# Sum passes of a two-layer graph network by groups of four blocks on one Trainium2 core

## The chip, the cores and the metric

The kernel runs on one core of one Trainium2 chip (trn2). The metric is the device time of one execution in microseconds (us). The engines are called PE (TensorE), DVE (VectorE), ACT (ScalarE), POOL (GpSimd) and SP (SyncE); each has its own instruction stream, and they meet only at semaphores.

## What is computed

12500 nodes with 64 features, 200000 edges (`src`, `dst`, sorted by `dst`). Three layers each sum the neighbours' states over the edges, and a fourth block sums the neighbours' states the other way and three edge features besides. Between them stand small matrix products and layer norms.

```python
def _demo_layer(h, src, dst, deg_pos, inv_deg, Wg, Wl, Ws, b):
    g = h @ Wg
    neigh_mean = jax.ops.segment_sum(h[dst], src, num_segments=h.shape[0]) * inv_deg[:, None]
    extra = neigh_mean @ Wl + h @ Ws
    out = g + deg_pos[:, None] * extra + b
    return jax.nn.elu(out)
...
    target_vec = jnp.concatenate([node_feature[node_j], ef, et], axis=1)
    neighbor_emb = target_vec @ W1.T + b1
    neighbors_sum = jax.nn.relu(jax.ops.segment_sum(neighbor_emb, node_i, num_segments=N))
    out = jnp.concatenate([neighbors_sum, source_node_vec], axis=1) @ W2.T + b2
```

## The kernel before, in words

**Setup.** The edges are ranked and scattered once, so that each block of 128 slots x 4 edges (`K = 4`) belongs to one tile of 128 nodes. There are 544 blocks (`NB`) in each of two orders, by source tile and by destination tile. The node states stay in SBUF in `node`; a state is kept as three bf16 parts side by side (`HW = 192` columns).

**The stages.** After the setup and two wide passes (`wide_by_dst`, `wide_by_src`) the program runs: node layer 1, spread, sums, layer 2, spread, sums, layer 3, spread, sums, spread, sums, and the last node block. A `spread` writes the states of 544 blocks into the table `gathered` in HBM. A `sums` reads them back in the other order and adds them up by node. `sums` is called four times, and it alone is changed, with the `gather` on POOL that feeds it.

**One `sums` stage** loops over 34 turns of 16 blocks (`TURN = 16`), and 4 blocks are a group, so a turn has 4 groups and a stage 136. For each block:
- POOL gathers 128 rows from `gathered` into one of 16 slots of `ring` (L641). It waits at the head of each group for the indices (`sum_idx`) and for each block until PE is done with the slot (`sum_mm`).
- DVE builds the one-hots of the block's slots in one of four buffers `oh_s` by one compare (L1350), three blocks ahead.
- PE multiplies the one-hots with the gathered rows, 4 matmuls (one for each of `K`) that add up in one of four PSUM banks (L818). It waits for `sum_oh`, `sum_got` and `sum_red`, and signals `sum_mm`.
- DVE sums the three parts from PSUM into `red` (L1354, signal `sum_red`) and adds `red` to the node's tile (L1468, signal `sum_add`). Where the tile lies is loaded into registers, eight at a time (L362).

**Beside it, once a group,** a quarter of the edge features is summed in fp32. SP fetches the rows into `frows` (L508). DVE builds their one-hots `foh` by a compare (L1350, called from `sums`) in its step for the first block of the group; ACT casts them to fp32 into `fohf` (L1083), which lies in `hring`, and then copies the next gather indices (L972). PE multiplies behind the fourth block of the group (`feature_sum`, L750, recorded as eight matmuls), and DVE adds the result to the node (L1444) in its step for the third block of the next group.

Nothing is scheduled by a planner: each engine's order is the order of the code, and inside an engine nothing overtakes.

Of the kernel before, what the change touches and what calls it, by code (L numbers as in the profile page):

```python
# [7 lines left out]
ALU = mybir.AluOpType  # L8
ACT = mybir.ActivationFunctionType
AX = mybir.AxisListType  # L10
# [5 lines left out]
P = 128  # L16
D = 64
# [52 lines left out]
def build(nc, x, src, dst, ef, stf, et, Wg1, Wl1, Ws1, b1, Wg2, Wl2, Ws2, b2, Wgo, Wlo, Wso, bo,  # L70
          W1t, c1, W2t, c2, out):
    with ExitStack() as ctx:
# [48 lines left out]
        red = sb("red", [P, 2, D])  # L121
# [76 lines left out]
        foh = sb("foh", [P, P, K], BF16)  # L198
        fohf = hring[:, :, :].rearrange("p s w -> p (s w)").bitcast(F32)[:, 0:K * P].rearrange("p (k n) -> p k n", n=P)
# [112 lines left out]
        class Sum:  # L312
# [3 lines left out]
            def __init__(self, number, k):  # L316
                self.k, self.q0, self.n0 = k, number * NQ, number * NB
                self.f0, self.g0 = number * NQ, (number + 2) * NI
                self.idx, self.got, self.oh = sum_idx, sum_got, sum_oh
                self.mm, self.red, self.add = sum_mm, sum_red, sum_add  # L320
# [242 lines left out]
        def _(pool):  # L563
# [65 lines left out]
            def gather(q, spread):  # L629
# [3 lines left out]
                def body(i, first):  # L633
                    for c in range(TURN):
                        n, g = TURN * i + (q.n0 + c), c // 4
# [17 lines left out]
        def _(pe):  # L653
# [155 lines left out]
            def sums(q):  # L809
                def body(i, first):  # L810
                    for c in range(TURN):
                        n = TURN * i + (q.n0 + c)
                        pe.wait_ge(q.oh, n + 1)
                        pe.wait_ge(q.got[c], 16 * i + (16 * q.g0 + 16))
                        if not first or c > 3:
                            pe.wait_ge(q.red, n - 3)
                        for k in range(K):
                            mm = pe.matmul(ps[:, c % 4, 0:HW], oh_s[:, c % 4, :, k], ring[:, c, k * HW:(k + 1) * HW],  # L818
                                           start=k == 0, stop=k == K - 1)
                        mm.then_inc(q.mm, 1)  # L820
                        if c % 4 == 3:
                            g = c // 4
                            f, u = 4 * i + (q.f0 + g), g % 2
                            pe.wait_ge(feat_ohf, f + 1)
                            pe.wait_ge(feat_row[u], 32 * i + (8 * q.f0 + (g // 2 * 16 + 16)))
                            if q.f0 > 0 or not first or g > 1:
                                pe.wait_ge(feat_add, f - 1)
# [839 lines left out]
```

## Time and profile before

| | |
|---|---|
| time, median of 2 runs | 11977.85 us (11972.17 to 11983.54) |
| profiled execution, its own time | 12008.01 us |
| span of that execution, first to last instruction | 12006.2 us |
| mean granted TensorE clock | 0.856 of 2.4 GHz |
| PE, DVE, POOL, ACT busy | 58%, 55%, 42%, 31% of the span |
| four `sums` stages | 544 blocks each |

Busy times are sums over a span; how full an engine is in one stage is read from a stretch of that stage. PE is the matmul row and PEld the weight loads that overlap it; matmuls are pipelined, and a row "x4" in order of time is four of them merged. In the rows in order of time the bracket is the idle time of the engine just before, with what ended it. "Remote" and "another core or an unknown queue" both mean that a semaphore came from something that the records of the moment do not name.

### The profile page before, as it was taken

How to read it: one execution, taken by the hardware profiler on the slowest of the kernel's cores; microseconds unless marked ns; L12 is line 12 of the kernel's file. 1: busy time of each engine (PE TensorE's matmuls, PEld its weight loads, DVE VectorE, ACT ScalarE, POOL GpSimd, SP SyncE). 2: the span in 40 equal slices, each digit the busy share in tenths (PEclk: the TensorE clock that was granted, in tenths of full speed). 3: DMA queues.
4: the chain of work that ended last, by engine and by line, in shares of the span. 5: the costliest groups of instructions: out<-in, count | busy, mean ns of one | idle time of the engine just before them, and what ended most of it. 6: DMA issues, size and time to landing. Idle time of an engine off the chain costs nothing.

```text
span 12006.2 us, 213561 instructions
## 1 busy us (share of the span) xinstructions
PE 7020.0 (58%) x46640; PEld 6056.7 (50%) x46640; DVE 6572.9 (55%) x19818; ACT 3664.2 (31%) x10935; POOL 5053.8 (42%) x4833
## 2 busy tenths in 40 slices
PE   7999998000049997545565555555536555655556
PEld 6898886000038886444344444444434444444445
DVE  8459998000046665444675456655567555665546
ACT  0003332000037775333571115811139211571111
POOL 0018888666644444554015550055500455215550
PEclk9999999999999998666797777977769777897776
DMA  9905555565569997455495564955629655885560
GB/s 385 366 20 144 145 144 142 137 148 137 144 194 304 301 301 225 142 142 135 165 346 161 164 164 155 358 164 163 160 52 395 201 163 160 269 333 161 164 161 18
DMA packets 1567398, 2320.70 MB, mean 193 GB/s; under 512 B 974516, under 2 KB 1046056, under 8 KB 1567320
## 3 DMA queue, kind: packets, MB, share of 16 engines
q1 hardware_dynamic: 1227608, 1356.73, 33.5%
q0 software_dynamic: 292608, 911.36, 27.5%
q10 hardware_dynamic: 47104, 51.75, 1.8%
q8 instruction: 27, 0.44, 0.0%
q14 instruction: 51, 0.42, 0.0%
HBM read 1328.55 MB, written 986.78 MB: 193 GB/s over the span
## 4 chain that ended last, share of the span: by engine, by line
PE 28%; issue 25%; DVE 19%; another core or an unknown queue 13%; ACT 7%; DVEq 4%; DMA 3%; ACTq 1%; POOL 0%; SPq 0%; POOLq 0%
PE ps L750 10%; PE ps L818 5%; PE ps L703 4%; DVE mask L1319 3%; DVE oh_s L1350 3%; ACT ring L1059 3%; DMA gathered<-ring 2%; PE ps L738 2%; ACT hring L1069 2%; PE ps L743 2%; DVE prod L1303 2%; PE ps L787 2%; DVEq L362 1%; DVE ohj L1209 1%
## 5 line engine op out<-in xcount | busy, mean ns | idle before, releaser
L641 POOL DMA_INDIRECT ring<-gathered,gidx x2176 | 2089.5, 960 | 3930.5 <-DMA gathered<-ring 2098.6
L571 POOL DMA_INDIRECT by_src<-prow,ppos x1562 | 1924.9, 1232 | 1485.5 <-DMA ppos<-pos 940.6
L818 PE MATMUL ps<-ring,oh_s 128*128 128x192 bf16 x8704 | 1217.8, 294 | 1797.3 <-DVE oh_s L1350 1585.3
L1354 DVE TENSOR_REDUCE red<-ps 128x64 f32<-128x192 f32 x2720 | 957.1, 352 | 2351.2 <-remote 1285.1
L818 PEld LDWEIGHTS ps<-ring,oh_s 128*128 128x128 bf16 x8704 | 918.6, 127 | 2059.2 <-DVE oh_s L1350 961.0
L1083 ACT CAST hring<-foh 128x512 f32<-128x512 bf16 x544 | 361.2, 664 | 3585.7 <-DVE foh L1350 3065.2
L1432 DVE CAST ring<-ps 128x384 bf16<-128x384 f32 x2176 | 1126.8, 553 | 328.1 <-PE ps L743 274.1
L743 PE MATMUL ps<-hring,oht_g 128*128 128x192 bf16 x8704 | 941.8, 246 | 544.7 <-DVE ring L1432 150.1
L750 PE MATMUL ps<-frows,hring 128*128 128x193 f32 x4352 | 1182.6, 433 | 4.2 <-issue 3.9
L1059 ACT CAST ring<-ps 128x384 bf16<-128x384 f32 x2176 | 1138.4, 524 | 10.1 <-PE ps L743 9.8
L1350 DVE TENSOR_TENSOR oh_s<-loc,iota_loc 128x512 bf16<-128x512 bf16 x2720 | 1126.5, 414 | 5.3 <-ACT loc L1027 3.1
L743 PEld LDWEIGHTS ps<-hring,oht_g 128*128 128x128 fp8e4 x8704 | 654.2, 97 | 832.2 <-issue 803.5
L721 PE MATMUL ps<-snap,oht_e 98*128 98x98 f32 x3130 | 1057.0, 441 | 0.0
L738 PE MATMUL ps<-ident_bf,oh 128*128 128x128 bf16 x2176 | 211.4, 220 | 1410.1 <-DVE oh L1350 1410.0
L750 PEld LDWEIGHTS ps<-frows,hring 128*128 128x128 f32 x4352 | 1008.9, 260 | 39.1 <-issue 6.8
L738 PEld LDWEIGHTS ps<-ident_bf,oh 128*128 128x128 bf16 x2176 | 167.9, 114 | 1410.7 <-issue 1410.6
L956 ACT COPY snap<-ps 98x98 f32<-98x98 f32 x1565 | 378.2, 242 | 1641.2 <-PE ps L718 1180.6
L1069 ACT COPY hring<-node 128x192 bf16 x2176 | 860.6, 396 | 55.3 <-issue 51.3
L750 PE MATMUL ps<-rows,ohf 128*128 128x193 f32 x4352 | 849.4, 339 | 26.6 <-ACT ohf L983 22.8
L604 POOL DMA_INDIRECT rows<-by_src,gidx x544 | 517.7, 952 | 727.3 <-PE ps L750 269.9
L721 PEld LDWEIGHTS ps<-snap,oht_e 98*128 98x128 f32 x3130 | 820.5, 323 | 0.0
L1338 DVE MEMSET node<- 128x64 f32 x1 | 0.1, 112 | 1356.1 <-DMA by_src<-prow,ppos 1356.1
(217 smaller groups left out, 12841.3 us busy)
## 6 DMA issues: line engine op xcount, KB each, us to landing
gathered<-ring SPq DMA_DIRECT2D x544, 768.0 KB
by_src<-zeros SPq DMA_DIRECT2D x34, 6272.0 KB, 45.5
frows<-by_src SPq DMA_DIRECT2D x544, 392.0 KB
oht_g<-oht SPq DMA_DIRECT2D x544, 256.0 KB, 5.4
gathered<-got SPq DMA_DIRECT2D x136, 776.0 KB
prow<-in_edge_attr_n SPq DMA_DIRECT2D x284, 352.0 KB
bc<-tidrow ACTq DMA_DIRECT2D x313, 160.0 KB
prow<-in_edge_attr SPq DMA_DIRECT2D x142, 352.0 KB
```

The source lines that it names most:

```text
L571: pool.indirect_dma_start(out=table, out_offset=bass.IndirectOffsetOnAxis(ap=ppos[:, s, j:j + 1], axis=0), in_=prow[:, s, j, :], in_offset ...
L641: pool.indirect_dma_start(out=ring[:, c, :], out_offset=None, in_=gb, in_offset=offsets(g, c % 4)).then_inc(q.got[c], 16)
L721: pe.matmul(where, oht_e[0:T, v, l * P:(l + 1) * P], snap[0:T, (u * LANES + l) % 2, :], start=True, stop=False, skip_group_check=True).the ...
L738: mm = pe.transpose(to[:, k * P:(k + 1) * P], one_hots[:, :, k], ident_bf[:, :])
L743: mm = pe.matmul(ps[:, bank + k // 2, k % 2 * HW:(k % 2 + 1) * HW], eight(one_hots)[:, k * P:(k + 1) * P], parts, start=True, stop=True, s ...
L750: mm = pe.matmul(ps[:, bank, 0:FEAT], one_hots[:, k, :], rows_of[:, k, 0:FEAT], start=k == 0, stop=k == K - 1)
L818: mm = pe.matmul(ps[:, c % 4, 0:HW], oh_s[:, c % 4, :, k], ring[:, c, k * HW:(k + 1) * HW], start=k == 0, stop=k == K - 1)
L1059: act.copy(ring[:, c, 0:2 * HW], ps[:, 2 * (c % 4), 0:2 * HW]).then_inc(q.g, 1)
L1069: act.copy(hring[:, e, :], parts_at(at[e])).then_inc(q.hc, 1)
L1350: return dve.tensor_tensor(to, loc[k][:, bass.ds(b * K, K)].unsqueeze(1).to_broadcast([P, P, K]), iota_loc[:, :, :], ALU.is_equal)
L1354: return dve.tensor_reduce(red[:, u], ps[:, bank, 0:HW].rearrange("p (a d) -> p d a", d=D), AX.X, ALU.add)
L1432: dve.tensor_copy(ring[:, c, 2 * HW:4 * HW], ps[:, 2 * (c % 4) + 1, 0:2 * HW]).then_inc(q.gv, 1)
```

## The change

The sum passes go by groups. `red` becomes two times four parts. Instead of four compares, four sums of parts and four PE signals, a group has one each. The one-hots of blocks move from `oh_s` to `oht_g` (`ohq`, two halves of four blocks); `oh_s` becomes free for two `foh` buffers and for the second of two `fohf`. PSUM banks 0 and 1 hold one group, 2 and 3 the next. One semaphore per group (`sum_got[::4]`) counts the four gathers. POOL waits for the slots once a group.

```diff
@@ buffers
-        red = sb("red", [P, 2, D])
...
-        foh = sb("foh", [P, P, K], BF16)
-        fohf = hring[:, :, :].rearrange("p s w -> p (s w)").bitcast(F32)[:, 0:K * P].rearrange("p (k n) -> p k n", n=P)
+        red = sb("red", [P, 2, 4, D])
+        ohq = oht_g[:, :, :].rearrange("p b s -> p (b s)").rearrange("p (e n k) -> p e n k", n=P, k=K)
+        foh = [oh_s[:, 2], oh_s[:, 3]]
+        fohf = [flat_of[:, 0:K * P].rearrange("p (k n) -> p k n", n=P) for flat_of in
+                (hring[:, :, :].rearrange("p s w -> p (s w)").bitcast(F32),
+                 oh_s[:, 0:2].rearrange("p a n k -> p (a n k)").bitcast(F32))]
@@ gather, POOL
                         if c % 4 == 0:
                             pool.wait_ge(q.idx, 4 * i + (q.q0 + g + 1))
-                        if not first:
-                            pool.wait_ge(q.mm, n - (TURN - 1))
+                            if not first:
+                                pool.wait_ge(q.mm, 4 * i + (q.q0 + g - 3))
...
-                                                in_offset=offsets(g, c % 4)).then_inc(q.got[c], 16)
+                                                in_offset=offsets(g, c % 4)).then_inc(q.got[g], 16)
@@ sums, PE
-                    for c in range(TURN):
-                        n = TURN * i + (q.n0 + c)
-                        pe.wait_ge(q.oh, n + 1)
-                        pe.wait_ge(q.got[c], 16 * i + (16 * q.g0 + 16))
-                        if not first or c > 3:
-                            pe.wait_ge(q.red, n - 3)
-                        for k in range(K):
-                            mm = pe.matmul(ps[:, c % 4, 0:HW], oh_s[:, c % 4, :, k], ring[:, c, k * HW:(k + 1) * HW],
-                                           start=k == 0, stop=k == K - 1)
+                    for g in range(4):
+                        m, f, u = 4 * i + (q.q0 + g), 4 * i + (q.f0 + g), g % 2
+                        pe.wait_ge(q.oh, m + 1)
+                        pe.wait_ge(q.got[g], 64 * i + (q.g0 + 64))
+                        if not first or g > 1:
+                            pe.wait_ge(q.red, m - 1)
+                        for e in range(4):
+                            c = 4 * g + e
+                            for k in range(K):
+                                mm = pe.matmul(ps[:, 2 * u + e // 2, e % 2 * 256:e % 2 * 256 + HW], ohq[:, c % 8, :, k],
+                                               ring[:, c, k * HW:(k + 1) * HW], start=k == 0, stop=k == K - 1,
+                                               skip_group_check=True)
                         mm.then_inc(q.mm, 1)
...
+                        pe.wait_ge(feat_ohf, f + 1)
+                        pe.wait_ge(feat_row[u], 32 * i + (8 * q.f0 + (g // 2 * 16 + 16)))
+                        if q.f0 > 0 or not first or g > 1:
+                            pe.wait_ge(feat_add, f - 1)
+                        feature_sum(4 + u, fohf[u], frows[:, u]).then_inc(feat_mm, 1)
@@ sums, ACT
-                        if q.f0 > 0 or not first or g > 0:
-                            act.wait_ge(feat_mm, f)
-                        act.copy(fohf, foh[:, :, :].rearrange("p n k -> p k n")).then_inc(feat_ohf, 1)
+                        if q.f0 > 0 or not first or g > 1:
+                            act.wait_ge(feat_mm, f - 1)
+                        act.copy(fohf[g % 2], foh[g % 2][:, :, :].rearrange("p n k -> p k n")).then_inc(feat_ohf, 1)
@@ sums, DVE
+                def ones(m, g):
+                    places = loc[q.k][:, bass.ds(m * (4 * K), 4 * K)].rearrange("p (e k) -> p e k", k=K)
+                    dve.tensor_tensor(ohq[:, 4 * (g % 2):4 * (g % 2) + 4], places.unsqueeze(2).to_broadcast([P, 4, P, K]),
+                                      iota_loc[:, :, :].unsqueeze(1).to_broadcast([P, 4, P, K]),
+                                      ALU.is_equal).then_inc(q.oh, 1)
...
+                        dve.wait_ge(q.mm, m + 1)
+                        dve.tensor_reduce(
+                            red[:, u], ps[:, 2 * u:2 * u + 2, :].rearrange("p b (h c) -> p (b h) c", c=256)[:, :, 0:HW]
+                            .rearrange("p e (a d) -> p e d a", d=D), AX.X, ALU.add).then_inc(q.red, 1)
+                        if not (last and g > 1):
+                            ones(4 * i + (g + 2), g)
+                        if q.f0 > 0 or not first or g > 1:
+                            dve.wait_ge(feat_ohf, f - 1)
+                        one_hots(foh[u][:, :, :], 1, f).then_inc(feat_oh, 1)
+                        dve.wait_ge(q.red, m + 1)
+                        for e in range(4):
+                            n = TURN * i + (q.n0 + 4 * g + e)
+                            if not first or g + e > 0:
+                                dve.wait_ge(q.add, n)
+                            to = node_at(at[4 * u + e], A0, D)
+                            dve.tensor_tensor(to, to, red[:, u, e], ALU.add).then_inc(q.add, 1)
+                        if not first or g > 0:
+                            features(f - 1, 1 - u, at_f[g - 1 if first else g], q.f0 == 0 and first and g == 1)
```

On PE, in the looped turn of the first `sums` stage, the second group of a turn stands like this before, with the features of the group (L750) behind its four blocks and each block waiting for its own signals:

```order
L813 REGISTER_ALU
L818 MATMUL ps<-ring,oh_s 128x192 [waits sum_red,sum_got4,sum_oh]
L818 MATMUL ps<-ring,oh_s 128x192 x3
L813 REGISTER_ALU
L818 MATMUL ps<-ring,oh_s 128x192 [waits sum_red,sum_got5,sum_oh]
L818 MATMUL ps<-ring,oh_s 128x192 x3
L813 REGISTER_ALU
L818 MATMUL ps<-ring,oh_s 128x192 [waits sum_red,sum_got6,sum_oh]
```

And so the same group in the changed kernel, with the features (L755) and the next group behind it:

```order
L821 REGISTER_ALU [waits sum_got4,sum_oh]
L825 MATMUL ps<-ring,oht_g 128x192 [waits sum_red]
L825 MATMUL ps<-ring,oht_g 128x192 x15
L755 MATMUL ps<-frows,oh_s 128x193 [waits feat_add,feat_row1,feat_ohf]
L755 MATMUL ps<-frows,oh_s 128x193 x3
L825 MATMUL ps<-ring,oht_g 128x192 [waits sum_red,sum_got8,sum_oh]
L825 MATMUL ps<-ring,oht_g 128x192 x15
```

The four waits of a group have become one, ahead of 16 matmuls in a row; the features stand behind the group and ahead of the next one in both.

On DVE, the head of a group in the looped turn of a later `sums` stage is this before; the first compare is that of `foh`, the second that of a block's one-hots:

```order
L1354 TENSOR_REDUCE red<-ps 128x64 [waits sum_mm]
L1458 REGISTER_ALU
L1350 ISA [waits feat_ohf]
L1350 TENSOR_TENSOR foh<-loc,iota_loc 128x512
L1350 ISA
L1350 TENSOR_TENSOR oh_s<-loc,iota_loc 128x512
L1468 ISA [waits sum_add,sum_red]
L1468 TENSOR_TENSOR node<-node,red 128x64
```

After the change the head of a group is this; the compare into `oht_g` is that of four blocks, the one into `oh_s` that of `foh`:

```order
L1462 TENSOR_REDUCE red<-ps 128x256 [waits sum_mm]
L1443 ISA
L1443 TENSOR_TENSOR oht_g<-loc,iota_loc 128x2048
L1354 ISA [waits feat_ohf]
L1354 TENSOR_TENSOR oh_s<-loc,iota_loc 128x512
L1474 REGISTER_ALU [waits sum_red]
L1476 ISA [waits sum_add]
L1476 TENSOR_TENSOR node<-node,red 128x64
```

The wait for `sum_mm` was that for the first block of the group and is now that for all four, and `foh` stands behind the reduce and the compare of four blocks.

## Rows read from the trace of the kernel before

**Rows 1.** The page, its head: span, busy time and share of each engine.
```profile
span 12006.2 us, 213561 instructions
...
PE 7020.0 (58%) x46640; PEld 6056.7 (50%) x46640; DVE 6572.9 (55%) x19818; ACT 3664.2 (31%) x10935; POOL 5053.8 (42%) x4833
```

**Rows 2.** Busy time by stretches: first and last `sums` stage, third node layer.
```profile
core 0: us, PE busy (x) PEld busy (x) DVE busy (x) ACT busy (x) POOL busy (x), PEclk, DMA share, GB/s
...
6266.00:7253.00 987.00, 552.03 (x3267) 478.94 (x3268) 508.20 (x1905) 106.75 (x276) 501.62 (x525) 0.74 0.57 159
...
10736.00:11722.00 986.00, 548.18 (x3231) 476.18 (x3231) 495.98 (x1880) 101.43 (x265) 516.80 (x538) 0.73 0.58 162
...
8763.00:9010.00 247.00, 77.05 (x410) 69.75 (x410) 159.86 (x307) 100.87 (x182) 0.00 (x0) 0.61 0.12 37
```

**Rows 3.** Groups by line within 700 us of the first `sums` stage.
```profile
L1350 DVE TENSOR_TENSOR oh_s<-loc,iota_loc 128x512 bf16<-128x512 bf16 x385 | 159.6, 414 | 0.0
...
L1354 DVE TENSOR_REDUCE red<-ps 128x64 f32<-128x192 f32 x385 | 135.4, 352 | 304.6 <-remote 145.5 <-PE ps L818 111.0 <-issue 47.9
...
L1083 ACT CAST hring<-foh 128x512 f32<-128x512 bf16 x96 | 63.7, 664 | 625.4 <-DVE foh L1350 534.1 <-issue 91.2
```

**Rows 4.** In order of time, a turn of that stage: start, length, engine, line.
```profile
6700.52 0.66 ACT L1083 CAST hring<-foh 128x512 f32<-128x512 bf16 x1 [9.80 <-DVE foh L1350]
...
6700.87 0.35 DVE L1354 TENSOR_REDUCE red<-ps 128x64 f32<-128x192 f32 x1
...
6701.50 2.84 PE L750 MATMUL ps<-frows,hring 128*128 128x193 f32 x8
...
6701.61 0.35 DVE L1354 TENSOR_REDUCE red<-ps 128x64 f32<-128x192 f32 x1
...
6702.14 0.97 POOL L641 DMA_INDIRECT ring<-gathered,gidx  x1 [4.74 <-PE ps L818]
...
6703.41 0.95 POOL L641 DMA_INDIRECT ring<-gathered,gidx  x1 [0.30 <-issue]
...
6704.13 2.80 PE L818 MATMUL ps<-ring,oh_s 128*128 128x192 bf16 x16
...
6706.72 1.58 PE L750 MATMUL ps<-frows,hring 128*128 128x193 f32 x8
...
6708.15 1.15 PE L818 MATMUL ps<-ring,oh_s 128*128 128x192 bf16 x12
...
6711.13 0.95 POOL L641 DMA_INDIRECT ring<-gathered,gidx  x1 [0.30 <-issue]
...
6713.73 0.36 DVE L1354 TENSOR_REDUCE red<-ps 128x64 f32<-128x192 f32 x1 [5.02 <-remote]
```

**Rows 5.** Busy time and clock in three short stretches of that turn.
```profile
6700.00:6704.00 4.00, 3.12 (x12) 3.01 (x13) 3.16 (x13) 0.76 (x2) 1.56 (x2) 0.50 0.24 86
6707.00:6709.00 2.00, 2.00 (x19) 1.95 (x19) 1.71 (x7) 0.00 (x0) 1.35 (x2) 1.00 0.61 209
6714.00:6718.00 4.00, 3.18 (x12) 3.01 (x13) 3.36 (x14) 0.76 (x2) 1.63 (x2) 0.50 0.39 111
```

**Rows 6.** The chain that ended last, in order of time, within that turn.
```profile
6704.34 0.65 PE ps L818 x4
...
6708.71 5.00 another core or an unknown queue
```

**Rows 7.** In order of time: the SyncE queue, and the next run of gathers.
```profile
6713.86 0.33 SPq L508 DMA_DIRECT2D frows<-by_src  x1
...
6716.07 0.98 POOL L641 DMA_INDIRECT ring<-gathered,gidx  x1 [3.99 <-PE ps L818]
...
6727.83 0.35 DVE L1444 TENSOR_TENSOR node<-node,ps 128x193 f32 x1 [2.29 <-remote]
```

**Rows 8.** Groups by line over the whole span, DVE operations of other sizes.
```profile
L1276 DVE TENSOR_TENSOR cmp<-iota_row,thr 99x512 f32<-99x512 f32 x272 | 188.2, 692 | 274.5 <-PE ps L703 274.5
...
L1416 DVE TENSOR_TENSOR node<-node,ps 128x1 f32 x544 | 79.9, 147 | 0.2 <-issue 0.2
...
L1494 DVE TENSOR_REDUCE nm<-oht_g 128x7 f32<-128x448 f32 x28 | 17.4, 622 | 1.0
```

More of the change, by code:

```diff
@@ L1435, in sums, with features @@
             def sums(q):
-                def ones(b, c):
-                    one_hots(oh_s[:, c % 4], q.k, b).then_inc(q.oh, 1)
-                def features(f, u, at):
+                def ones(m, g):
[3 more added lines that the diff above has]
+                                      ALU.is_equal).then_inc(q.oh, 1)
+                def features(f, u, at, first):
                     dve.wait_ge(feat_mm, f + 1)
-                    if not (isinstance(f, int) and f == 0):
+                    if not first:
                         dve.wait_ge(feat_add, f)
@@ L1446, in body @@
                 def body(i, first, last=False):
-                    at_f = tiles(1, 4 * i + q.f0, 4, mybir.EngineType.DVE)
-                    for half in range(2):
-                        at = tiles(q.k, TURN * i + 8 * half, 8, mybir.EngineType.DVE)
-                        for e in range(8):
-                            c = 8 * half + e
-                            n = TURN * i + (q.n0 + c)
-                            f, g = 4 * i + (q.f0 + c // 4), c // 4
-                            dve.wait_ge(q.mm, n + 1)
-                            parts_summed(c % 2, c % 4).then_inc(q.red, 1)
-                            if c % 4 == 0:
-                                if q.f0 > 0 or not first or g > 0:
-                                    dve.wait_ge(feat_ohf, f)
-                                one_hots(foh[:, :, :], 1, f).then_inc(feat_oh, 1)
-                            if not (last and c > TURN - 4):
-                                ones(TURN * i + (c + 3), c + 3)
-                            if c % 4 == 2 and g > 0:
-                                features(f - 1, (g - 1) % 2, at_f[g - 1])
-                            dve.wait_ge(q.red, n + 1)
-                            if not first or c > 0:
-                                dve.wait_ge(q.add, n)
-                            to = node_at(at[e], A0, D)
-                            dve.tensor_tensor(to, to, red[:, c % 2], ALU.add).then_inc(q.add, 1)
@@ L1469, in body @@
-                    features(4 * i + (q.f0 + 3), 1, at_f[3])
-                for b in range(3):
-                    ones(b, b)
+                    at_f = tiles(1, q.f0 if first else 4 * i + (q.f0 - 1), 4, mybir.EngineType.DVE)
+                    for g in range(4):
+                        m, f, u = 4 * i + (q.q0 + g), 4 * i + (q.f0 + g), g % 2
+                        if u == 0:
+                            at = tiles(q.k, TURN * i + 4 * g, 8, mybir.EngineType.DVE)
+                        dve.wait_ge(q.mm, m + 1)
[11 more added lines that the diff above has]
+                            if not first or g + e > 0:
+                                dve.wait_ge(q.add, n)
+                            to = node_at(at[4 * u + e], A0, D)
+                            dve.tensor_tensor(to, to, red[:, u, e], ALU.add).then_inc(q.add, 1)
+                        if not first or g > 0:
+                            features(f - 1, 1 - u, at_f[g - 1 if first else g], q.f0 == 0 and first and g == 1)
@@ L1472, in sums @@
+                for m in range(2):
+                    ones(m, m)
                 body(0, True)
@@ L1475, in sums @@
                 body(NI - 1, False, True)
+                at_f = tiles(1, q.f0 + NQ - 4, 4, mybir.EngineType.DVE)
+                features(q.f0 + NQ - 1, 1, at_f[3], False)
                 dve.wait_ge(q.add, NB + q.n0)
+                dve.wait_ge(feat_add, q.f0 + NQ)
             def spread_over(ap):
```

21 lines of the change are left out of this document (6 added, 15 removed).

## The prediction

> **What bounds the kernel now.** I read the page first, then the busy time by stretches, the groups of instructions inside one aggregation stage, and last two turns of that stage in order of time. The page gives a span of 12006.2 us, with no engine above 58% [rows 1]: nothing is full, so the time lies in waits between engines. The change touches only `sums`, which runs four times. The stretches [rows 2] show the first and the last of those stages alike: of 987 and 986 us PE is busy 552 and 548 us (56%), DVE and POOL about half, and the granted TensorE clock is 0.74 and 0.73. Since only 1.2 and 2.4 GHz are ever granted, a mean of 0.74 is some 48% of the time at 2.4 GHz.
>
> The groups in 700 us of the first stage [rows 3] give the pace: 96 casts of the feature one-hots on ACT, one for each group of four blocks, so 700/96 = 7.29 us a group. There are 4 stages x 136 groups = 544 groups; their 544 x 7.3 = 3970 us are a third of the span. In a group POOL issues 4 gathers in steps of 1.25 to 1.27 us [rows 4], 5.0 us; DVE has four steps of 0.73 and two instructions of some 0.35 more, 3.6 us. Both would allow a shorter group than 7.3.
>
> What fills it can be read in order of time [rows 4]. DVE's step for one block is reduce, one-hot, add, 0.73 us (6700.87 to 6701.61). PE's features at 1.2 GHz take 2.63 us (6701.50 to the next product at 6704.13); at 2.4 GHz they take 1.43 us (6706.72 to 6708.15), and a product 0.082 us instead of 0.16. That the clock is 0.50 there and 1.00 later stands in the stretches of a few us [rows 5]. Then comes a gap that no engine accounts for: PE's last product record begins before 6709.3, yet DVE's reduce, which waits only for PE's signal, begins at 6713.73 after 5.02 us. The chain calls the releaser unknown [rows 6], and the SyncE queue, which waits for the signal of the features that started at 6706.72, issues its next DMA at 6713.86 [rows 7]. All that time POOL had gathers running: it began at 6702.14, issued eight, the last at 6711.13. The product that ended at 6704.99 was answered at once [rows 6], those behind it late. The second run of gathers shows the same: begun at 6716.07, a late signal, of the features, seen at 6727.83 [rows 7]. I read this as: PE's signals are prompt in the first 3 us or so of a run of gathers, and are held after that until the run has nearly landed, 2.6 us after its last one began (6713.73 less 6711.13). The mechanism is not visible; the pattern is.
>
> **The change part by part.** On DVE four reduces become one of 768 inputs (L1462), four compares one of 2048 elements (L1443); the four adds, the feature compare and the feature add stay. PE signals once a group, POOL waits once a group, and PSUM and one-hots hold two groups. The price of the new operations:
> - Reduce: 192 inputs take 352 ns [rows 3] and 448 take 622 ns [rows 8], 1.055 ns more for each, so 768 take 0.96 us against 4 x 0.35. Bounds: 0.9 to 1.41 (four old ones).
> - Compare: a one-element add takes 147 ns [rows 8]; 512 bf16 elements take 414 [rows 3], so 0.52 ns an element and 1.22 us for 2048, against 4 x 0.41. If the four-level pattern lost that rate it would go by the fp32 compare, 692 ns for 512 (1.06 ns each, [rows 8]): 2.33 us. I take 1.22, since types and innermost run are those of before.
> - The saved signals and fixed parts, some 0.7 us of DVE a group, are work on an engine that waits half of the time: nothing by themselves. The moves of `foh` and `fohf` into other tiles and the second buffer of each cost nothing; neither does the single wait of POOL, whose 0.30 us between gathers is there when it waits for nothing [rows 4].
>
> **What the new order makes of it.** The products are said to run two groups ahead, and `oh` and PSUM would allow it. But the order of PE is products m, features m, products m+1, and features m wait for `feat_ohf`, which ACT makes from `foh`, and DVE makes `foh` of group m only behind its wait for the products of the same group m, and now behind the large reduce and the large compare. Before, DVE made it after the first block of the group, and PE still had three blocks, whose cover the change takes away. So PE is never ahead, and a group is one chain without overlap: products m, signal, reduce, compare, `foh`, ACT's cast, features m, products m+1. Its links, from [rows 4] where not priced above:
> - DVE and ACT: reduce 0.88 and compare 1.14 (each less the 0.08 by which the next one overlaps), `foh` 0.42, cast 0.66, and hand-overs 0.02 + 0.04 + 0.05: 3.2 us.
> - PE at 1.2 GHz: features 2.63, products 4 x 0.65 [rows 6] = 2.60, and 0.2 from the last product's turn to its signal: 5.4. At 2.4 GHz: 1.43 + 16 x 0.082 = 1.31 + 0.2: 2.95.
> - So a group is 8.6 us at 1.2 GHz and 6.15 at 2.4 GHz, if signals are prompt.
> - The held signals: ACT copies the next indices right behind the cast; POOL's first gather starts 0.96 us after the cast's end (6701.18 to 6702.14). The signal of the next products is due 5.45 us after the cast at 1.2 GHz, 4.5 into POOL's run, and 3.0 at 2.4 GHz, 2.0 into it. The first falls where signals were held. A run is now four gathers, 3 x 1.25 us from first start to last start, and over 2.6 later: 6.35. That holds the slow case's signal another 1.85: 10.45 us. The fast case is not held. Bounds for the hold: 0 to 3 us.
>
> Which clock? PE would be busy 5.2 of 10.45 us in the slow case and 2.75 of 6.15 in the fast one, about 48%. The busy share and the clock go together in the trace: 56% with 0.74, and 77 of 247 us, 31%, with 0.61 [rows 2]. Between them 48% gives 0.70, 40% of the time at 2.4 GHz. The mean group is then 1/(0.6/10.45 + 0.4/6.15) = 8.17 us. Against 7.29 this is 0.88 us more, x 544 = 479 us. Nothing outside `sums` changes. The profiled execution took 12008.0 us, 30 above the median of 11977.9: 12008 + 479 - 30 = 12,457, I say 12,460 us.
>
> **The rivals.**
> - *Full clock throughout.* What speaks for it: at 2.4 GHz PE's idle piece is only 3.2 us a group, shorter than the one of over 4.5 us behind which the clock fell [rows 4, 5], and all of PE's work of a group is in one piece. Against it: PE is busy less than now, and a lower share goes with a lower clock [rows 2]. Each group takes 6.15: 544 x -1.14 = -620, 11,360 us. It decides from about three quarters of the time at 2.4 GHz, where the group is 6.85. The Trainium skill (TensorE: Matmul & The Clock Gate, HAM oscillation) says that gaps in the matmuls are what brings the clock down, and by that rule this rival gains; the gap of this trace, from before 6709.3 until the clock is back at 0.50, agrees, and no row here has a steady train of 3.2 us ones. Chance 0.17.
> - *Signals not held.* Runs of four with a pause, and a quarter of PE's signals, may keep every signal prompt. Then 1/(0.6/8.6 + 0.4/6.15) = 7.41 us, +65: 12,040 us, no change. For it: the first signals of both runs were prompt. Against it: 4.5 us into a run none is seen prompt. Chance 0.21.
> - *Compare at the fp32 rate.* The chain gets 1.11 longer: 9.28 us, 13,060 us. Chance 0.07.
> - *Clock at 1.2 GHz throughout.* 10.45 us a group, 13,690 us. Chance 0.07.
> - That it does what its name says, PE really ahead by two groups, would leave POOL's 5.0 us as the bound and give -1200. The order of instructions excludes it.
>
> **How the numbers follow.** My forecast, the chain at mixed clock with held signals, has 0.48; its own range is 12,200 to 12,850. Measurement can tell about 2%, 240 us. Faster: the first rival and a little from the second's lower edge, 0.20. Within 2%: most of the second and the low edge of the forecast, 0.21. Slower: the rest, 0.59. The range reaches down to 11,550, half of the first rival, and up to 13,300, past the slow compare; outside are some 0.09 and 0.07.
>
> **What would show it.** In the changed profile: no products of a group before the features of the last one; ACT's cast waiting for DVE's `foh`, and PE's features waiting for the cast, in every group; casts every 8 us rather than 7.3; the compare at 1.2 us and the reduce at 0.96; POOL in runs of four with pauses of 3 us; a mean clock near 0.70; the spread and node stages unchanged. I am wrong if PE's features do not wait for the cast, if groups come under 7 us, or if the clock is above 0.85 in these stages.

## The result, and the profile after

The changed kernel took 12,493.19 us (two runs, 12,484.01 to 12,502.37) where the kernel before took 11,977.85: a ratio of 1.043, 95% interval 1.0385 to 1.0475, slower. The forecast was 12,460 us, a ratio of 1.040, by +0.88 us a group. The profiled execution took 12,484.01 us. It is the first case forecast, slower, and 33 us from the median; but two of its terms were wrong, in opposite directions, and the experiments below are there to separate them.

The head of the page of the kernel after, and its row for the gathers, against [rows 1]:

```profile
span 12482.2 us, 198644 instructions
...
PE 7395.1 (59%) x46640; PEld 6501.7 (52%) x46640; DVE 6479.0 (52%) x16554; ACT 3659.7 (29%) x10935; POOL 5028.2 (40%) x4833
...
L646 POOL DMA_INDIRECT ring<-gathered,gidx x2176 | 2063.1, 948 | 4474.9 <-DMA gathered<-ring 2129.8
```

There are 14,917 instructions fewer, and DVE is busy 94 us less. PE, with exactly as many matmuls as before, is busy 375 us longer: they ran at a lower clock. Busy time by stretches for the first and the last `sums` stage of the kernel after, as in [rows 2]:

```profile
6224.00:7211.00 987.00, 589.11 (x2901) 526.33 (x2900) 430.10 (x961) 89.25 (x240) 456.51 (x483) 0.71 0.48 145
11100.00:12087.00 987.00, 585.81 (x2894) 523.01 (x2895) 431.87 (x967) 90.00 (x242) 456.60 (x482) 0.71 0.48 145
```

In as many microseconds PE gets through 2901 recorded matmuls where it had 3267. The groups by line, kernel after, 6400 to 7100 us, as in [rows 3]:

```profile
L755 PE MATMUL ps<-frows,oh_s 128*128 128x193 f32 x344 | 119.7, 525 | 137.5 <-ACT oh_s L1088 134.3 <-issue 3.2
...
L1443 DVE TENSOR_TENSOR oht_g<-loc,iota_loc 128x2048 bf16<-128x2048 bf16 x86 | 104.6, 1216 | 0.0
L1462 DVE TENSOR_REDUCE red<-ps 128x256 f32<-128x768 f32 x86 | 82.4, 958 | 360.1 <-PE ps L825 211.8 <-issue 148.4
```

86 groups in 700 us are 8.14 us each; over a whole stage, from its first cast to its last, the groups of the four stages take 8.25, 8.23, 8.26 and 8.24 us, where before they took 7.31, 7.34, 7.34 and 7.33. 544 groups by 0.91 us are 495 us, and that is the whole difference (476 between the two profiled executions, 515 between the medians). The new operations cost what was forecast: the compare 1.216 us, the reduce 0.958. PE now waits for ACT's cast, which it did not before. And DVE's reduce waits for nothing that is unknown: the 145.5 us of "remote" in [rows 3] are gone.

In order of time, kernel after, two groups (start, length, engine, line, and in brackets the idle time before):

```profile
6706.42 2.91 PE L755 MATMUL ps<-frows,hring 128*128 128x193 f32 x8 [3.46 <-ACT hring L1088]
...
6707.12 0.95 POOL L646 DMA_INDIRECT ring<-gathered,gidx  x1 [3.00 <-ACT gidx L977]
...
6709.12 2.77 PE L825 MATMUL ps<-ring,oht_g 128*128 128x192 bf16 x16
...
6710.87 0.95 POOL L646 DMA_INDIRECT ring<-gathered,gidx  x1 [0.30 <-issue]
6711.93 0.96 DVE L1462 TENSOR_REDUCE red<-ps 128x256 f32<-128x768 f32 x1 [4.92 <-issue]
6712.80 1.22 DVE L1443 TENSOR_TENSOR oht_g<-loc,iota_loc 128x2048 bf16<-128x2048 bf16 x1
6713.94 0.42 DVE L1354 TENSOR_TENSOR oh_s<-loc,iota_loc 128x512 bf16<-128x512 bf16 x1
...
6714.39 0.65 ACT L1088 CAST oh_s<-oh_s 128x512 f32<-128x512 bf16 x1 [8.12 <-DVE oh_s L1354]
...
6715.09 2.78 PE L755 MATMUL ps<-frows,oh_s 128*128 128x193 f32 x8 [3.20 <-ACT oh_s L1088]
...
6717.67 1.99 PE L825 MATMUL ps<-ring,oht_g 128*128 128x192 bf16 x16
...
6719.69 0.96 DVE L1462 TENSOR_REDUCE red<-ps 128x256 f32<-128x768 f32 x1 [3.75 <-PE ps L825]
...
6723.05 2.91 PE L755 MATMUL ps<-frows,hring 128*128 128x193 f32 x8 [3.39 <-ACT hring L1088]
```

This is the serial chain of the forecast, link by link. Features 2.70 us (6706.42 to 6709.12; forecast 2.63), products and their signal 2.81 (forecast 2.80), reduce to features 3.16 (6711.93 to 6715.09; forecast 3.2): 8.67 us from features to features, where the forecast had 8.6 for a group at 1.2 GHz with prompt signals. The signal comes 4.8 us into POOL's run of four, where the forecast had it held by 1.85 us. It was not held: the reduce begins as soon as PE's last product is over (6709.12 + 2.77 = 6711.89, and 6711.93). So it is all through this stage: in 128 of 129 groups between 6240 and 7300 us the reduce begins 0.04 us after the end of the last product's record. The next group, 6715.09 to 6723.05, takes 7.96.

The clock of the same two groups, by stretches of the kernel after (PE busy is the second number, the granted clock the third from the end):

```profile
6703.00:6706.30 3.30, 0.00 (x0) 0.00 (x0) 3.01 (x6) 0.74 (x2) 0.94 (x1) 0.81 0.74 253
6706.40:6709.10 2.70, 2.68 (x8) 2.56 (x9) 0.57 (x2) 0.00 (x0) 1.67 (x2) 0.50 0.14 24
6709.10:6711.90 2.80, 2.79 (x17) 2.27 (x15) 0.00 (x0) 0.00 (x0) 2.11 (x3) 0.51 0.76 238
6712.00:6715.00 3.00, 0.00 (x0) 0.00 (x0) 2.71 (x5) 0.61 (x2) 0.00 (x0) 1.00 0.41 139
6715.10:6717.60 2.50, 2.50 (x8) 2.40 (x9) 0.70 (x3) 0.03 (x1) 1.31 (x2) 0.54 0.00 0
6717.70:6719.60 1.90, 1.90 (x17) 1.67 (x15) 0.00 (x0) 0.00 (x0) 1.42 (x2) 0.74 0.74 142
```

Here is the second thing that the forecast had wrong. The mean is 0.71 (forecast 0.70), but the full clock falls mostly on the stretches in which PE waits (1.00 from 6712 to 6715, with no matmul at all), and the low one on those in which it works. Laid over PE's matmul records of the stage (6224 to 7211 us), the clock record is at 2.4 GHz in 81% of PE's idle time and in 15% of its busy time; in the kernel before (6266 to 7253) it is at 2.4 GHz in 43% of the busy time. The mean while PE works has fallen from 0.71 to 0.58, while the mean over the whole stretch has only fallen from 0.74 to 0.71. Of the 128 groups from 6240 to 7300, 77 take 7.6 to 8.2 us and 51 take 8.7 to 8.9; none is near the 6.15 us that I had given to 40% of the time.

### The profile page after: what moved, and what is told of

Same layout as the page of the kernel before. It is cut to its first block, busy times and chain, and to the rows that moved or that the text cites. A ratio compares the mean times of both kernels' runs of the same rounds, so it can differ in the third digit from the quotient of the medians.

```text
span 12482.2 us, 198644 instructions
## 1 busy us (share of the span) xinstructions
PE 7395.1 (59%) x46640; PEld 6501.7 (52%) x46640; DVE 6479.0 (52%) x16554; ACT 3659.7 (29%) x10935; POOL 5028.2 (40%) x4833
## 4 chain that ended last, share of the span: by engine, by line
PE 32%; issue 31%; DVE 17%; ACT 7%; DMA 4%; DVEq 3%; another core or an unknown queue 3%; ACTq 1%; POOL 0%; SPq 0%; POOLq 0%
PE ps L755 13%; PE ps L825 6%; PE ps L708 4%; DMA gathered<-ring 4%; DVE mask L1323 3%; PE ps L743 3%; ACT ring L1064 2%; DVE oh_s L1354 2%; PE ps L748 2%; ACT hring L1074 2%; PE ps L792 2%; DVE prod L1307 1%; DVE ohj L1213 1%; PE ps L670 1%
## 5 line engine op out<-in xcount | busy, mean ns | idle before, releaser
L1462 DVE TENSOR_REDUCE red<-ps 128x256 f32<-128x768 f32 x544 | 521.1, 958 | 2347.6 <-PE ps L825 1523.6
L755 PE MATMUL ps<-frows,hring 128*128 128x193 f32 x2176 | 754.8, 525 | 927.3 <-ACT hring L1088 900.3
L825 PE MATMUL ps<-ring,oht_g 128*128 128x192 bf16 x8704 | 1257.7, 324 | 53.8 <-DMA ring<-gathered,gidx 53.8
L755 PE MATMUL ps<-frows,oh_s 128*128 128x193 f32 x2176 | 741.2, 516 | 913.4 <-ACT oh_s L1088 887.7
L1436 DVE CAST ring<-ps 128x384 bf16<-128x384 f32 x2176 | 1094.0, 552 | 360.0 <-PE ps L748 332.7
L748 PE MATMUL ps<-hring,oht_g 128*128 128x192 bf16 x8704 | 886.5, 247 | 598.9 <-DVE ring L1436 219.1
L825 PEld LDWEIGHTS ps<-ring,oht_g 128*128 128x128 bf16 x8704 | 1138.2, 139 | 194.3 <-issue 145.7
L755 PEld LDWEIGHTS ps<-frows,hring 128*128 128x128 f32 x2176 | 624.8, 312 | 993.8 <-issue 979.8
L755 PEld LDWEIGHTS ps<-frows,oh_s 128*128 128x128 f32 x2176 | 603.9, 303 | 989.9 <-ACT oh_s L1088 962.5
L755 PE MATMUL ps<-rows,ohf 128*128 128x193 f32 x4352 | 846.8, 338 | 27.9 <-ACT ohf L988 23.8
L1088 ACT CAST oh_s<-oh_s 128x512 f32<-128x512 bf16 x272 | 176.4, 648 | 2091.3 <-DVE oh_s L1354 2091.3
```

Of the source, the lines that this page charges most:

```text
L748: mm = pe.matmul(ps[:, bank + k // 2, k % 2 * HW:(k % 2 + 1) * HW], eight(one_hots)[:, k * P:(k + 1) * P], parts, start=True, stop=True, s ...
L755: mm = pe.matmul(ps[:, bank, 0:FEAT], one_hots[:, k, :], rows_of[:, k, 0:FEAT], start=k == 0, stop=k == K - 1)
L825: mm = pe.matmul(ps[:, 2 * u + e // 2, e % 2 * 256:e % 2 * 256 + HW], ohq[:, c % 8, :, k], ring[:, c, k * HW:(k + 1) * HW], start=k == 0, ...
L1436: dve.tensor_copy(ring[:, c, 2 * HW:4 * HW], ps[:, 2 * (c % 4) + 1, 0:2 * HW]).then_inc(q.gv, 1)
L1462: dve.tensor_reduce(red[:, u], ps[:, 2 * u:2 * u + 2, :].rearrange("p b (h c) -> p (b h) c", c=256)[:, :, 0:HW] .rearrange("p e (a d) -> p ...
```

## The experiments

One thing must be said first: the runs were made in four sessions, and the kernel before did not take the same time in all of them. In two sessions (e1 to e4; e10 and r4) it took 10,502.52 and 10,502.45 us; in the two others (r1, r2, e5, e6; e7 and e8) 11,984.12 and 12,015.88, as in the result above. I call the first two sessions A and the other two B. A kernel is compared only with the kernel before of its own session.

**e1, session A.** `foh` of group f+1 is built in the step of group f, so PE's features never wait for the reduce and the compare of their own group.

```
-  if q.f0 > 0 or not first or g > 1:
-      dve.wait_ge(feat_ohf, f - 1)
-  one_hots(foh[u][:, :, :], 1, f).then_inc(feat_oh, 1)
+  if not (last and g == 3):
+      if q.f0 > 0 or not first or g > 0:
+          dve.wait_ge(feat_ohf, f)
+      one_hots(foh[1 - u][:, :, :], 1, f + 1).then_inc(feat_oh, 1)
...
+  one_hots(foh[0][:, :, :], 1, q.f0).then_inc(feat_oh, 1)
```

> The changed kernel, in which DVE builds the feature one-hots of group m+1, not of group m, in its step for group m. Nothing is left out. Chain theory: features m no longer wait for anything that comes behind products m, so a group falls from 8.2 us to what is next, a run of four gathers with the held signal behind it, about 6.6 us: 544 x (6.6 - 8.2) = -870, about 11,620 us. If no signal is held, PE and POOL set it at 5.3 us: about 10,900. Rival (the large DVE operations or the lower clock cost the time, not the order): unchanged, 12,490 us within 1%.

Measured: 10,674.20 us (four runs), ratio to before 1.0157, interval 1.014 to 1.0174. The 11,620 us that I had expected counted on late signals, of which session A shows none; without them I had expected 10,900. **e2, session A**, leaves `foh` in its group but moves its two statements ahead of the large reduce, directly behind the wait for the products:

```
   dve.wait_ge(q.mm, m + 1)
+  if q.f0 > 0 or not first or g > 1:
+      dve.wait_ge(feat_ohf, f - 1)
+  one_hots(foh[u][:, :, :], 1, f).then_inc(feat_oh, 1)
   dve.tensor_reduce(
...
   ones(4 * i + (g + 2), g)
-  if q.f0 > 0 or not first or g > 1:
-      dve.wait_ge(feat_ohf, f - 1)
-  one_hots(foh[u][:, :, :], 1, f).then_inc(feat_oh, 1)
```

> The changed kernel, in which the feature one-hots of group m stand ahead of the large reduce and the large compare of the same step, still behind the wait for products m. Nothing is left out. Chain theory: the chain of a group gets shorter by the reduce and the compare, 0.88 + 1.14 = 2.0 us, in the slow case from 10.45 to 8.4, in the fast one to the 5.3 us of POOL and PE; mean near 6.5: about 11,570 us. Rival (order does not matter): 12,490 us.

Measured: 10,684.47 us (one run). Groups by line of e1, 5800 to 6500 us:

```profile
L646 POOL DMA_INDIRECT ring<-gathered,gidx x497 | 527.6, 1062 | 173.7 <-issue 146.4 <-PE ps L825 22.1 <-ACT gidx L977 5.2
...
L1443 DVE TENSOR_TENSOR oht_g<-loc,iota_loc 128x2048 bf16<-128x2048 bf16 x122 | 148.7, 1218 | 0.0
...
L755 PE MATMUL ps<-frows,oh_s 128*128 128x193 f32 x488 | 113.5, 385 | 15.3 <-DVE node L1452 9.3 <-ACT hring L1088 3.4 <-issue 2.6
```

122 groups in 700 us, 5.74 each; in this row PE's wait for the cast has shrunk from 134 us to 3.4. Over whole stages the groups of e1 take 5.78 to 5.86 us. With all the rest of the change kept (one reduce, one compare, one signal a group), moving `foh` alone takes 2.4 us off each group, against the 8.17 of the changed kernel on such a chip (r4 below). So nearly all of the loss lies in where `foh` stands, and not in the large operations or the rarer signals: e1 takes back 1312 of the 1484 us by which the changed kernel is slower in session A. The other 172 us, 1.6%, remain, and no run here says what they are; the nearest bound is POOL, at (1.062 + 0.30) x 4 = 5.45 us a group.

**e3, session A**: the kernel before with the gathers of the `sums` stages left out (`gather` does nothing, PE and ACT do not wait for it). **e10**, the same kernel in another session A. **e4, session A**: the changed kernel with the same left out. The sums are then of what happens to be in the ring. The lines below are those of e4.

```
   def gather(q, spread):
-      ...
+      pass
...
-  pe.wait_ge(q.got[g], 64 * i + (q.g0 + 64))
...
-  act.wait_ge(q.got[g], 64 * i + (q.g0 + 64))
+  act.wait_ge(q.idx, 4 * i + (q.q0 + g + 1))
```

> The kernel before without the gathers of its four sum stages: POOL issues none, nobody waits for one, and the products use what lies in the ring. All other work stays. Theory of held signals: without gathers PE's signals are prompt, the 5 us gaps go, and a group falls from 7.3 to about 4.6 us (DVE's 3.6 as the floor, PE's chain of 5.0 at the low clock): 544 x -2.7 = -1,470, about 10,500 us. Rival (the gaps have another cause, such as a change of PE's clock): about 11,980 us, gaps of 3 to 5 us before DVE's reduce still there.

> The changed kernel without the gathers of its four sum stages, in the same way. Theory: the chain without overlap stays, only the hold of up to 1.85 us in the slow case goes: 8.2 becomes about 7.4 us a group, about 12,060 us, and by no means under 6.15 us a group (11,380). It is then slower than the kernel before without gathers by 2.8 us a group, 1,500 us. Rival (the changed kernel is slow because of held signals): it falls as far as the kernel before, to 10,500.

> The kernel before without the gathers of its four sum stages, once more, since e3 ran on a chip on which the signals were not late in the first place. On a chip of the slower kind (kernel before at 11,980 us): theory of signals held while gathers land: without gathers a group takes the same 4.3 us as in e3, 544 x (4.3 - 7.34) = -1,650, about 10,330 us. Rival (the slower chip's PE is late by itself): the group stays well over 5 us and the kernel over 10,800. On a chip of the faster kind: 9,820 again.

Measured: e3 9822.32 us, groups of 4.28 us, 680 less than before; e10 9827.37, 675 less. e4 11,944.29 us, 42 less than r4. e4 by stretches and by line:

```profile
6000.00:6700.00 700.00, 418.52 (x2059) 374.37 (x2058) 304.43 (x680) 63.26 (x170) 0.00 (x0) 0.71 0.16 49
```

```profile
L742 PE MATMUL ps<-frows,oh_s 128*128 128x193 f32 x344 | 119.6, 525 | 137.5 <-ACT oh_s L1074 137.5
...
L1448 DVE TENSOR_REDUCE red<-ps 128x256 f32<-128x768 f32 x85 | 81.4, 958 | 355.6 <-PE ps L811 355.6
```

Without a single gather the changed kernel has the same pace (8.17 us), the same clock and the same wait of PE for the cast, 137.5 us. I had expected the groups to shorten when the gathers went; that theory fell here. By itself e4 speaks for session A alone; that there was no hold in the result either is read from its own trace, above. For the same reason e3 and e10 do not test whether gathers make signals late: the 1470 us that I had expected e3 to save were late signals, and no trace of session A has them. e3 gives an estimate for the group of the kernel before in session A, of which there is no trace: 4.28 + (10,502 - 9822)/544 = 5.5 us, if all of the difference lies in the `sums` stages.

**r4, session A**: the changed kernel itself.

> The changed kernel, unchanged. On a chip of the slower kind 12,490 again. On a chip of the faster kind (kernel before at 10,500 us), where it was not yet run: the chain does not depend on the chip, 8.2 us a group as in e4, about 11,960 us, 14% slower than the kernel before there. Rival (the chain gains from that chip as much as the kernel before): 10,950.

Measured: 11,986.48 us against 10,502.45, one run each: 14.1% slower, groups of 8.15 to 8.19 us. The change costs 544 x 2.7 us there and 544 x 0.9 here. The groups of the changed kernel hardly differ between the sessions (8.17 and 8.24 us); it is the kernel before whose groups are so much shorter in A (some 5.5 us against 7.33). So the forecast of 4% could be right only where the kernel before has its late signals.

**r1 and r2, session B**: both kernels once more, where the kernel before took as long as in the result.

> The kernel before, unchanged, for its trace on the chip of these runs, where its median was 10,502 us and not 11,978. Theory: what is different is the held signals. If they are missing here, DVE's reduce is not late by 3 to 5 us, and a group of a sum stage takes about 5.4 us in place of 7.3 (4 x 136 x 1.9 = 1,030 us of the 1,475 less), with the rest in the two wide passes; engine durations are the same. Rival: the chip's engines or DMA are simply faster, every stage shorter in the same ratio of 0.877.

> The changed kernel, unchanged, on the same chip as the others. Chain theory: a group is the chain of products, reduce, compare, foh, cast and features and hardly depends on gathers or on held signals; it took 8.2 us without gathers, so it takes about 8.25 us here too and the kernel about 12,000 us, 14% slower than the kernel before on the same chip. Rival (both are limited by the same thing and 4% is the price everywhere): 10,950 us.

Measured: before 11,991.73, after 12,499.23 (four runs), ratio 1.0428, interval 1.041 to 1.0445: the result again. Both expectations had counted on a session like A, so that r2 came out 500 us above its own, nearly all of it ahead of the `sums` stages. The waits of r1, 6400 to 7100 us (total, times, longest):

```profile
DVE red L1354 <- remote: 128.6, 29, 5.5
DVE node L1444 <- remote: 102.3, 22, 5.4
```

The late signals of [rows 3, 6, 7] are there again, 231 us in 96 groups. In the traces of e1, e2 and r4 from session A there are none within the `sums` stages.

**e5, session B**: the changed kernel, with 16 products of constants behind each group's products, into a PSUM bank that nothing reads, so that PE has work while it would wait for the cast.

```
   mm.then_inc(q.mm, 1)
+  for k in range(16):
+      pe.matmul(ps[:, 6, 0:HW], ident_bf[:, :], iota_loc[:, 0:HW // K, :].rearrange("p n k -> p (n k)"),
+                start=True, stop=True, skip_group_check=True)
   pe.wait_ge(feat_ohf, f + 1)
```

> The changed kernel with 16 more matmuls a group into an unused PSUM bank, on constants, between the products and the wait for the feature one-hots, so in time in which PE idles. Clock theory: the mean group of 8.2 us lies between a chain of 8.7 at 1.2 GHz and 6.2 at 2.4 GHz; if the extra work keeps the clock at 2.4 GHz a group takes about 6.4, 544 x -1.8 = -980 against the changed kernel on the same chip, about 11,000. Rival (the clock is set otherwise or does not matter): not faster, up to 0.3 us a group slower where the extra matmuls do not fit the gap.

Measured: 11,825.29 us (one run): 674 less than r2 and 1.3% less than before, by adding work. e5 by stretches, and in order of time:

```profile
6400.00:7100.00 700.00, 492.05 (x4071) 457.54 (x4069) 365.19 (x816) 75.87 (x204) 409.58 (x409) 0.90 0.60 172
```

```profile
6504.55 2.83 PE L755 MATMUL ps<-frows,hring 128*128 128x193 f32 x8 [2.14 <-issue]
...
6507.17 1.92 PE L825 MATMUL ps<-ring,oht_g 128*128 128x192 bf16 x16
...
6508.93 1.48 PE L830 MATMUL ps<-iota_loc,ident_bf 128*128 128x192 bf16 x16
...
6512.28 1.57 PE L755 MATMUL ps<-frows,oh_s 128*128 128x193 f32 x8 [1.88 <-ACT oh_s L1091]
...
6513.70 1.48 PE L825 MATMUL ps<-ring,oht_g 128*128 128x192 bf16 x16
```

Both kinds of group stand in these rows: features and products in 4.5 us, and in 2.9. Of 108 groups from 6300 to 7050, 64 take 6.1 to 6.3 us and 38 take 7.7 to 8.1. So the 6.15 us of the forecast for a group at 2.4 GHz is the right price of a thing that the changed kernel does not reach by itself. I had expected nearly all groups there, 6.4 us in the mean, and 11,000 us; a third of them stay slow. PE still stands idle some 2 us a group; that this is why is not shown.

**e6, session B**: in the kernel before, only `foh` is moved, from the first block of a group to the last (`if c % 4 == 0:` becomes `if c % 4 == 3:`).

> The kernel before with one move: DVE builds the feature one-hots of a group in its step for the last block of the group, not for the first. Nothing is left out, and no operation changes its size. Chain theory: the missing cover alone makes it slow: products of the last blocks, signal, reduce, foh, cast and features stand in a row, some 6.9 us at 1.2 GHz and 4.4 at 2.4 GHz where the four products are done at once, near 6.5 us a group with the mixed clock, +550 to +600 us against the kernel before on this chip (11,080). Rival (only the large operations cost): no change, 10,500.

Measured: 12,107.90 us (one run), +124, 0.23 us a group, a quarter of what I had expected from the numbers of session A. Its waits, 6400 to 7100 us:

```profile
PE ps L750 <- ACT hring L1083: 216.6, 88, 4.6
DVE red L1354 <- PE ps L818: 210.4, 77, 4.1
```

PE's wait for the cast appears, 2.5 us in 88 groups, as in the changed kernel. But the waits of the reduce for "remote" have nearly gone in exchange (3.6 us, against 128.6 in r1). The chain is longer, and the late signals that it replaces can have paid for most of it. The change costs 0.9 us a group in B and 2.7 in A, so the same exchange seems to hide a large part of its cost too.

**e8, session B**: the kernel of e1 again. **e7, session B**: the same, with the large compare cut into four of 512 elements, one ahead of each add.

```
+  if not (last and g > 1):
+      ones(4 * i + (g + 2), g, [e])       # one block's 512 elements
   to = node_at(at[4 * u + e], A0, D)
   dve.tensor_tensor(to, to, red[:, u, e], ALU.add).then_inc(q.add, 1)
```

> e1 with one more edit: the compare of 2048 elements is four of 512 again, one ahead of each add of a part. Nothing is left out. Theory: e1's group of 5.8 us is POOL's pace, 4 gathers of 1.25 us plus 0.47 us for each one that a compare of 2048 covers (1418 against 945 ns), while gathers beside a compare of 512 took 987 ns in the kernel before. Short compares then give 5.2 to 5.4 us a group on the faster chip: 10,400 us, 1% under the kernel before and 2.5% under e1. On the slower chip, where signals set the pace, e7 and e8 within 1%. Rival (the longer gathers come from the traffic of the DMA engines): e7 not faster than e8 anywhere.

> The kernel of e1 once more, beside e7. On a chip like that of e1 (kernel before at 10,500 us): 10,675 as then. On a chip like that of the first comparison (kernel before at 11,980 us), where PE's signals are late while gathers land: the lost cover is back, so a group falls well under the changed kernel's 8.24 us; each signal can cost until the run of four gathers has landed, 6.4 us after its start, so a group is 6.4 to 7.3 us and the kernel 11,480 to 11,980. Rival (the chain is not the cause): 12,490 there.

Measured: e7 11,475.52 us (four runs), ratio to before 0.9554, interval 0.9538 to 0.957; e8 11,486.53. Both have groups of 6.40 us. They beat the kernel before by 4.5% and, by the ratios to it, the changed kernel by some 8%; so at the pace of the result, too, the loss is gone when `foh` is built ahead. That they differ by 0.1% says that the length of the compare does not matter in B. Why 6.4 here and 5.8 in A, with the same kernel? First e8, then e1, in order of time:

```profile
6501.76 2.66 PE L825 MATMUL ps<-ring,oht_g 128*128 128x192 bf16 x16
...
6504.53 0.95 POOL L646 DMA_INDIRECT ring<-gathered,gidx  x1 [0.30 <-issue]
...
6507.10 0.96 DVE L1462 TENSOR_REDUCE red<-ps 128x256 f32<-128x768 f32 x1 [4.27 <-remote]
```

```profile
6208.76 2.75 PE L825 MATMUL ps<-ring,oht_g 128*128 128x192 bf16 x16 [3.81 <-DMA ring<-gathered,gidx]
...
6210.62 0.95 POOL L646 DMA_INDIRECT ring<-gathered,gidx  x1 [0.30 <-issue]
...
6211.55 0.96 DVE L1462 TENSOR_REDUCE red<-ps 128x256 f32<-128x768 f32 x1 [3.89 <-PE ps L825]
```

In e8 PE is done at 6504.42 and DVE learns of it at 6507.10, 2.57 us after the last gather of the run began; the forecast read 2.6 off the kernel before. Of the 67 reduces between 6266 and 7090 us before which DVE stood idle for over 2 us, 55 waited for such a signal, and in the median they began 2.56 us after the start of the latest gather. In e1, also within a run of gathers, PE is done at 6211.51 (6208.76 + 2.75), and DVE starts at 6211.55. So late signals exist, in sessions B and with long runs of gathers, and in e1 runs as long have none.

## Why the prediction was right, and where it was not

- *PE is not ahead, and a group is one chain*: right. Between 6400 and 7100 us after the change the cast waits for `foh` in all 86 groups, and PE waits for the cast in 84 of 85. e1 takes `foh` out of the chain, e2 moves it ahead of the reduce and the compare, and the loss is gone but for 1.6 to 1.7% (in B, with e8, it becomes a gain of 4.4%).
- *Prices on DVE*, 0.96 and 1.22 us: measured 0.958 and 1.216. The rival with the compare at the fp32 rate was never in play.
- *Links at 1.2 GHz, 8.6 us*: measured 8.67. *At 2.4 GHz, 6.15*: e5's short groups take 6.1 to 6.3.
- *The held signals*: wrong. "That holds the slow case's signal another 1.85: 10.45 us" should have been 0, within the bounds of 0 to 3. "The first falls where signals were held" took a time within a run of eight and applied it to a run of four with a pause behind it. The result's own trace shows the signal at once in 128 of 129 groups, and e4, in session A, no difference without gathers. The rival "signals not held" had this right, and its 7.41 us a group was too low for the other reason, the clock.
- *Which clock*: the mean was right (0.71 for 0.70) and its use wrong. "40% of the time at 2.4 GHz" was shared out over whole groups, fast ones of 6.15 and slow ones. But a mean over time counts the stretches in which PE idles at the full clock. PE had the full clock in 15% of its busy time only. In most groups the features took the 2.7 us of 1.2 GHz, in a fifth of them 2.0 to 2.2; the products took from 1.6 us, near the full clock, to 2.8. No group had both short, so the groups took 7.6 to 8.2 or 8.7 to 8.9 us. PE's busy share was 59 to 60%, not 48%: the hold, which would have been idle time, was missing (5.2 of 8.6 us are 60%), and the slow matmuls filled more of each group. Here a higher share went with a lower clock, against the line that the forecast drew through [rows 2].
- The two errors: with no hold and the forecast's clock, 7.41; with no hold and the clock as it was, 8.24; with both as forecast, 8.17. The total came out right because they cancel. The order of operations and its prices were foreseen; that the sum met the measured time within 33 us was luck.
- *POOL in runs of four with pauses of 3 us*: right, 3.00 to 4.2 us.
- *Full clock throughout*: PE had a gap of some 3.3 us in each group, and the full clock in 15% of its busy time; in e5, where the gaps are some 2 us, it had it in 73% (6300 to 7050 us, the added products included), and gained 674 us. The Trainium skill (TensorE: Matmul & The Clock Gate, HAM oscillation) says that gaps in the matmuls bring the clock down. The trace agrees with that direction, but not with what the forecast drew from it, that this rival gains with gaps of 3.2 us. This rival was given 0.17; its price was right (e5's short groups), its condition not met.

What stays open: why signals are late in sessions B and prompt in sessions A. Within B the lateness goes with gathers in long runs (there in before, r1, e7, e8; not in after, hardly in e6), but the gathers were never taken out in a session B, so that they cause it is argued, not shown. Neither is it known whether A and B are a property of the chip: the results number the chip 5 and 11 in the sessions A, and 15 and 11 in the sessions B, so if the same number means the same chip, one chip has shown both. e7 was not run in a session A, where POOL is the limit and short compares may help; e1 with the idea of e5 was not tried.

## What to carry to other kernels

When operations of several blocks are merged, look for the small step that another engine waits for between them: merged or not, it should not stand behind the large ones, and is best built one group ahead. Running ahead is only real if every producer in the ring is ahead: here one-hots and products were, and the feature one-hot pulled them all back into one chain. And do not turn a mean granted clock into a share of fast work, before looking in which stretches the engine works.

## What was not expected of the hardware

**Two kinds of sessions.** The kernel before took 10,502 us in some and 11,984 or 12,016 in others, 14% apart, with every single run within 0.2% of its session's median. In the changed kernel (11,986 against 12,493) 457 of the 507 us lie ahead of the first cast of the first `sums` stage, which is at 5747 us in A and at 6204 in B.

**Gathers wait for large compares.** A gather's issue takes 0.95 us alone. From e2 in order of time:

```profile
6205.49 1.22 DVE L1443 TENSOR_TENSOR oht_g<-loc,iota_loc 128x2048 bf16<-128x2048 bf16 x1
6205.87 1.65 POOL L646 DMA_INDIRECT ring<-gathered,gidx  x1 [0.30 <-issue]
...
6210.09 1.22 DVE L1443 TENSOR_TENSOR oht_g<-loc,iota_loc 128x2048 bf16<-128x2048 bf16 x1
...
6210.43 1.70 POOL L646 DMA_INDIRECT ring<-gathered,gidx  x1 [0.30 <-ACT gidx L977]
```

Both end 0.81 to 0.82 us after the end of the compare in which they began (7.52 less 6.71, 12.13 less 11.31). In e1, 542 gathers began within such a compare, and in the median they ended 0.82 us after it. This lengthens the mean gather of e1 to 1.062 us (0.948 in the changed kernel, where pauses keep the two apart), 0.46 us of POOL's time a group. The Trainium skill (SBUF — State Buffer, "SBUF: two separate sides") says that VectorE, in some of its instructions, and GpSimd share a port pair which one holds for its whole instruction while the other blocks, and that the descriptors of a DMA from the GpSimd queue are written through it. The trace agrees in kind: a fixed time after the compare's end, not a proportional slowing; the compare keeps its 1.22 us. It does not agree in size: the page gives some 115 ns after the end of VectorE's instruction, and here it is 0.81 to 0.82 us.

**The recorded clock of the setup.** Row PEclk of the page and the row of one matmul, first of the kernel after as profiled for the result, then of r2, the same kernel:

```profile
PEclk5555555555599997667977769777678777987776
...
L726 PE MATMUL ps<-snap,oht_e 98*128 98x98 f32 x3130 | 1056.9, 441 | 0.0
```

```profile
PEclk9999999999999997777977769777678777987776
...
L726 PE MATMUL ps<-snap,oht_e 98*128 98x98 f32 x3130 | 1056.8, 441 | 0.0
```

The first 11 slices are recorded at 0.5 in one and at 0.9 or more in the other, and the matmuls of this row, which lie within them (830 to 2057 us), take 441 ns in both. So for the setup that record says nothing, and neither does a mean clock of the whole program (0.703 and 0.841 in the two runs of the result, 0.15% apart in time). Where the clock is read, the duration of a matmul must bear it out, as it does in the `sums` stages.
